# Gate and turn of a fused Mamba, BitLinear, attention and feed-forward kernel written out step by step, with the rounding of quantised rows on ScalarE

## The reference

```python
x = x + tanh(g_xattn[0]) * mamba(ctx, z=layernorm(x))       # scan over 16 states, then y * silu(z)
x = x + tanh(g_ffn[0])   * bitlinear_ffn(layernorm(x))      # w1, exact gelu, w2
x = x + tanh(g_xattn[1]) * attention(layernorm(x), ctx)     # softmax of q k^T over channels
x = x + tanh(g_ffn[1])   * ffn(layernorm(x))                # 2048 wide, exact gelu
# in bitlinear, per row of x:
scale = 127.0 / max(max(abs(x)), EPS)
x_quant = clip(round(x * scale), -128.0, 127.0) / scale
# in mamba, per channel and state n:
state = state * exp(dt * A) + (dt * u) * B;  y += state * C
```

## Time and profile before

| | us |
|---|---|
| median of 3 runs | 1057.2 (1055.8 to 1058.83) |
| the profiled execution | 1057.6 |
| its span, first to last instruction | 1055.8 |
| busy: TensorE, VectorE, ScalarE, GpSimd | 823.3, 824.9, 665.5, 564.1 |
| mean granted clock of TensorE, share of full | 0.896 |

### The profile page before, as it was taken

The page is one execution under the profiler, slowest core; times in us unless marked ns, Lnnn a source line. Parts: engine busy times, 40 slices in busy tenths (PEclk is TensorE's granted clock), DMA queues, the critical chain, the costliest instruction groups (busy, mean ns, idle before and its releaser), DMA issues.

```text
span 1055.8 us, 10904 instructions
## 1 busy us (share of the span) xinstructions
PE 823.3 (78%) x2704; PEld 399.7 (38%) x2704; DVE 824.9 (78%) x1001; ACT 665.5 (63%) x972; POOL 564.1 (53%) x493
## 2 busy tenths in 40 slices
PE   5442320699699987989699988889799988898998
PEld 2110110344334334444334334344333434445887
DVE  4879968887988897687998898777998897764333
ACT  4679969366589962365589962565599852533442
POOL 0398785123997783123997783134997782133000
PEclk9555555799899999998999999998999999999999
DMA  7069985001199897201199897201298995200222
GB/s 276 0 119 205 231 195 107 0 1 41 22 190 206 189 251 179 77 26 40 20 198 201 191 246 179 102 0 40 50 204 184 203 219 155 99 1 21 94 90 76
DMA packets 51439, 130.07 MB, mean 123 GB/s; under 512 B 6304, under 2 KB 7456, under 8 KB 50864
## 3 DMA queue, kind: packets, MB, share of 16 engines
q0 software_dynamic: 17280, 62.92, 32.4%
q1 hardware_dynamic: 34096, 66.53, 18.6%
HBM read 62.33 MB, written 4.19 MB: 63 GB/s over the span
## 4 chain that ended last, share of the span: by engine, by line
PE 27%; DVE 21%; issue 17%; ACT 13%; DMA 9%; POOL 8%; DVEq 1%; ACTq 0%; POOLq 0%
DMA u<-work 9%; DVE pair L1194 7%; PE bank L630 4%; PE pair L514 4%; PE pair L630 4%; POOL work L1600 4%; PE bank L615 3%; DVE pair L1207 3%; PE pair L542 3%; ACT pair L825 2%; ACT L825 2%; PE bank L602 2%; ACT L1074 2%; PE pair L591 1%; POOL u L1611 1%
## 5 line engine op out<-in xcount | busy, mean ns | idle before, releaser
L1600 POOL TENSOR_TENSOR work<-du,bcast 128x1024 f32<-128x1024 f32 x128 | 346.8, 2736 | 54.0 <-DVE du L1256 45.6
L825 ACT ACTIVATE pair<-dt,a_neg 128x512 f32<-128x512 f32 x256 | 166.3, 683 | 63.3 <-DVE work L1199 52.6
L1194 DVE TENSOR_TENSOR_SCAN pair<-pair,work 128x512 f32<-128x512 f32 x160 | 186.9, 1214 | 16.3 <-ACT pair L825 15.7
L602 PE MATMUL bank<-stage,ring 128*128 128x512 f32 x384 | 174.8, 598 | 11.0 <-ACT stage L1074 3.7
L1611 POOL DMA_DIRECT2D u<-work x120 | 126.0, 1050 | 67.6 <-DVE work L1211 22.4
L423 PE MATMUL bank<-xd,pick 128*128 128x512 bf16 x128 | 56.9, 445 | 101.9 <-ACT bcast L810 66.1
L1207 DVE TENSOR_TENSOR_SCAN pair<-pair,work 128x512 f32<-128x512 f32 x96 | 117.4, 1223 | 18.1 <-ACT pair L825 17.7
L602 PEld LDWEIGHTS bank<-stage,ring 128*128 128x128 f32 x384 | 70.4, 189 | 96.4 <-issue 78.5
L1199 DVE TENSOR_TENSOR work<-pair,ccast 128x1024 f32<-128x1024 f32 x80 | 98.0, 1225 | 11.4 <-DVE pair L1194 6.1
L615 PE MATMUL bank<-ring,stage 128*128 128x512 f32 x192 | 88.8, 614 | 8.4 <-DVE stage L1476 7.0
L423 PEld LDWEIGHTS bank<-xd,pick 128*128 128x128 bf16 x128 | 13.1, 103 | 161.7 <-ACT bcast L810 101.0
(11 more groups left out here) (181 smaller groups left out, 1606.9 us busy)
## 6 DMA issues: line engine op xcount, KB each, us to landing
u<-work POOLq DMA_DIRECT2D x120, 512.0 KB, 5.7
ring<-ffn_dram SPq DMA_DIRECT2D x144, 256.0 KB, 5.0
ring<-ffn_dram SPq DMA_DIRECT2D x16, 512.0 KB, 3.3
xres<-x_dram SPq DMA_DIRECT2D x4, 1024.0 KB, 5.2
stage<-w_dram SPq DMA_DIRECT2D x1, 4096.0 KB, 17.4
stage<-w_dram SPq DMA_DIRECT2D x4, 1024.0 KB, 6.8
out_dram<-stage SPq DMA_DIRECT2D x16, 256.0 KB, 2.1
ctxT<-ctxT_dram SPq DMA_DIRECT2D x4, 512.0 KB, 6.4
```

Of the source, the lines that this page charges most:

```text
L602: last = pe.matmul(banks[2 + f % 2][:], piece(f)[:, k * P:(k + 1) * P], xnT[:, k, :], start=k == 0, stop=k == J - 1)
L825: act.activation(pairs[s % DECAYBUFS][:, q, :], dt[:, p * HALF + q, :], ACT.Exp, scale=a_neg[:, p * HALF + q, n:n + 1]).then_inc(s_decay, 1)
L1194: dve.tensor_tensor_scan(pair[:, q, :], pair[:, q, :], rows[:, q, :], 0.0, ALU.mult, ALU.add).then_inc(s_scan, 1)
L1600: pool.tensor_tensor(work[:, s % SCANBUFS, :, :], du[:, p * HALF:(p + 1) * HALF, :], bcast[:, n % 2, :].unsqueeze(1).broadcast_to([P, HALF ...
```

## The change

Slots 13 and 14 go, and their contents are written out as `turning` (and `first_turning` for pass 0) on each engine. Of the steps: both sums of the gate stand ahead of both products; the rounding's multiply-add is made by ScalarE (`q_scale`) between VectorE's `q_norm` and `q_out`; `x1n` has two buffers, for even and odd tiles; the mean for the gate's norm is made by ScalarE (`gate_mean`), not GpSimd; `gate_transposes` of tile 3 stand behind a pair of `f_down`, and the transposes of `q1`'s tile 1 ahead of the last pair; ScalarE copies tiles 2 and 3 before the last gelu. In `between`, `h_quant(b, 0)` stands ahead of `convolve(m, 1)`, `attend(b, 1)` ahead of `norm_transpose(b, 2)`, with ScalarE's copy of that ahead of its first copy of B.

```diff
-SLOTS = 15
+SLOTS = 13
...
-            (12, 0): (1, 2), (12, 1): (1, 4), (12, 3): (1, 6),
-            (13, 0): (1, 8), (13, 2): (1, 10), (13, 3): (1, 12),
-            (14, 0): (1, 14)}
-FOURTH_SLOTS = {(11, 0): 0, (14, 1): 1}
+            (12, 0): (1, 2), (12, 1): (1, 4), (12, 3): (1, 6)}
+FOURTH_SLOTS = {(11, 0): 0}
...
-        x1n = ccast[:, 0, :]
+        x1n = ccast
...
+            def f_pair(b, r, f):
+                f_down(b, r, f)
+                f_down(b, r, f + 1)
+
+            def first_turning(m):
+                pe.wait_ge(s_wq, 4)
+                gate_transposes(m, (0, 1, 2, 3))
+                q_transposes(m, (0,))
+                up1(m, 0)
+                q_transposes(m, (1,))
+                up1(m, 1, range(FC - 1))
+                q_transposes(m, (2,))
+                up1(m, 1, (FC - 1,))
+                q_transposes(m, (3,))
+
+            def turning(b, m):
+                f_pair(b, 1, 8)
+                gate_transposes(m, (0,))
+                gate_transposes(m, (1,))
+                gate_transposes(m, (2,))
+                f_pair(b, 1, 10)
+                gate_transposes(m, (3,))
+                f_pair(b, 1, 12)
+                q_transposes(m, (0,))
                 up1(m, 0, range(FC - 1))
-                if prev is not None:
-                    f_unit(prev, QUANT_SLOT, 0)
+                q_transposes(m, (1,))
+                f_pair(b, 1, 14)
                 up1(m, 0, (FC - 1,))
-                q_transposes(m, (1,))
...
+                if t == 1 and m is not None:
+                    pe.wait_ge(s_spmax, m * J + J)
...
                 attend(b, 0)
+                attend(b, 1, m)
                 norm_transpose(b, 2)
                 scan_bcast(m, 0, 0)
-                attend(b, 1)
-                norm_transpose(b, 3)
                 attend(b, 2)
                 scan_bcast(m, 1, 0)
+                norm_transpose(b, 3)
...
+                norm_copy(b, 2)
                 first_copy(m, b, 0, 0)
-                norm_copy(b, 2)
...
+            def gate_mean(b, j):
+                act.wait_ge(s_zsum, b * J + j + 1)
+                act.activation(zst[:, j, 1:2], zst[:, j, 0:1], ACT.Copy, scale=-1.0 / D).then_inc(s_zmean, 1)
...
+            def q_scale(b, t):
+                act.wait_ge(s_q1s, b * T + t + 1)
+                act.activation(x1n[:, t % 2, :], x1n[:, t % 2, :], ACT.Identity, scale=mst[:, t, 12:13],
+                               bias=expo[:, 2:3]).then_inc(s_q1m, 1)
+
+            def turning(m):
+                q_scale(m, 0)
                 q_copy(m, (0,))
-                gelu1(m, 0)
+                q_scale(m, 1)
+                gelu1(m, 0, range(FC - 2))
+                q_scale(m, 2)
                 q_copy(m, (1,))
+                gelu1(m, 0, range(FC - 2, FC))
+                q_scale(m, 3)
                 gelu1(m, 1, range(FC - 1))
                 q_copy(m, (2,))
+                q_copy(m, (3,))
                 gelu1(m, 1, (FC - 1,))
-                q_copy(m, (3,))
...
                 convolve(m, 0)
+                h_quant(b, 0)
                 convolve(m, 1)
-                h_quant(b, 0)
...
+            def first_turning(m):
+                last_sum(m, 0)
+                last_sum(m, 1)
+                gated(m, 0)
+                gated(m, 1)
+                first_sum(m, 0)
+                first_sum(m, 1)
+                q_norm(m, 0)
+                first_sum(m, 2)
+                q_norm(m, 1)
+                q_out(m, 0)
+                first_sum(m, 3)
+                q_out(m, 1)
+                q_norm(m, 2)
+                q_norm(m, 3)
+                q_out(m, 2)
+                q_out(m, 3)
+
+            def turning(b, m):
+                last_sum(m, 0)
+                last_sum(m, 1)
+                gated(m, 0)
+                gated(m, 1)
+                first_sum(m, 0)
+                first_sum(m, 1)
+                first_sum(m, 2)
+                q_norm(m, 0)
+                q_out(m, 0)
+                first_sum(m, 3)
+                q_norm(m, 1)
+                q_out(m, 1)
+                q_norm(m, 2)
+                q_norm(m, 3)
+                fourth(b, 1)
+                q_out(m, 2)
+                q_out(m, 3)
...
-            def quantise(b, t):
+            def q_norm(b, t):
                 st = mst[:, t, :]
+                row = x1n[:, t % 2, :]
                 dve.wait_ge(s_x1rs, b * T + t + 1)
-                if t:
-                    dve.wait_ge(s_q1, b * T + t)
+                if t >= 2:
+                    dve.wait_ge(s_q1, b * T + t - 1)
...
-                dve_m.link(dve, b, dve.reciprocal(st[:, 12:13], st[:, 11:12]))
+                dve.reciprocal(st[:, 12:13], st[:, 11:12]).then_inc(s_q1s, 1)
                 dve.tensor_scalar(st[:, 13:14], st[:, 11:12], wstat[:, 0, 2:3], None, ALU.mult)
-                dve_m.link(dve, b, dve.tensor_scalar(x1n, x1n, st[:, 12:13], MAGIC, ALU.mult, ALU.add))
+
+            def q_out(b, t):
+                dve.wait_ge(s_q1m, b * T + t + 1)
                 if t >= 2:
                     dve.wait_ge(s_q1T, b * T + t - 1)
-                dve.tensor_scalar(q1[:, t % 2, :], x1n, MAGIC, 127.0, ALU.subtract, ALU.min).then_inc(s_q1, 1)
+                dve.tensor_scalar(q1[:, t % 2, :], x1n[:, t % 2, :], MAGIC, 127.0, ALU.subtract, ALU.min).then_inc(s_q1, 1)
...
-                if slot == ZSTAT_SLOT - 1:
-                    for j in range(J):
-                        pool.wait_ge(s_zsum, b * J + j + 1)
-                        carry_wait(pool, "pool")
-                        pool.tensor_scalar(zst[:, j, 1:2], zst[:, j, 0:1], -1.0 / D, 1.0, ALU.mult,
-                                           ALU.mult).then_inc(s_zmean, 1)
```

More of the change, by code:

```diff
@@ L54 @@
 ZS_SLOT = 12
-GATE_SLOT = 13
-QUANT_SLOT = 14
 W_MEAN = {5: 0, 10: 1}
@@ L279, in program @@
         s_q1 = sem("s_q1")
+        s_q1s = sem("s_q1s")
+        s_q1m = sem("s_q1m")
         s_q1T = sem("s_q1T")
@@ L746, in pass_ @@
                 for slot in range(4, SLOTS):
-                    if slot == QUANT_SLOT:
-                        turn(m, prev)
-                        continue
                     bcast_next(m, slot, 0, 0)
@@ L760, in pass_ @@
                         weights(slot)
-                    if slot == GATE_SLOT:
-                        gate_transposes(m, range(T))
                     bcast_next(m, slot, 0, 1)
@@ L778, in pass_ @@
                         f_unit(b, slot, 3)
+                if rest:
+                    turning(b, m)
+                else:
+                    first_turning(m)
             def weights(slot):
@@ L1127, in pass_ @@
                         gates_silu(m)
-                    if slot == QUANT_SLOT:
-                        turn(m)
+                turning(m)
             def weights(slot):
@@ L1520, in pass_ @@
                     half(m, prev, slot, 1, 1)
-                    mixer_last(m, prev, slot)
-                    if rest and (slot, 1) in FOURTH_SLOTS:
-                        fourth(b, FOURTH_SLOTS[slot, 1])
+                if rest:
+                    turning(b, m)
+                else:
+                    first_turning(m)
             pass_(None, rest=False)
@@ L1640, in mixer_last, with turning @@
                                            ALU.mult).then_inc(s_zrs, 1)
-                if slot == GATE_SLOT:
-                    for t in range(T):
-                        st = mst[:, t, :]
-                        pool.wait_ge(s_x1st, b * T + t + 1)
-                        rsqrt(pool_m, b, st[:, 8:9], st[:, 7:8], LN_EPS, st[:, 9:10], s_x1rs)
+            def turning(b):
+                for t in range(T):
+                    st = mst[:, t, :]
+                    pool.wait_ge(s_x1st, b * T + t + 1)
+                    rsqrt(pool_m, b, st[:, 8:9], st[:, 7:8], LN_EPS, st[:, 9:10], s_x1rs)
             def norm(b, i):
```

34 lines of the change are left out of this document (11 added, 23 removed).

## The result

| | kernel before | changed kernel |
|---|---|---|
| median, us (20 executions each) | 1056.49 (1051.71 to 1059.73) | 1059.33 (1055.32 to 1065.78) |
| ratio | | 1.0035, 95% interval 1.0019 to 1.0051 |
| profiled execution, and its span | 1057.6, 1055.8 | 1058.4, 1056.6 |
| mean granted clock in it | 0.896 | 0.888 |

The two profiled executions differ by only 0.8 us: each is one draw from a spread of several microseconds. So single steps can be compared, not the ends; a second profile of the changed kernel (e12) shows how far a stage scatters by itself.

What follows compares the result with a forecast made beforehand. No engine was taken to bound the whole; the bound changes by stage, with ScalarE's last start counting at batches 2 and 3. 0.5 + 1.9 + 0.1 + 0.3 - 0.4 + 0.4 = +2.8 us gave 1060.0 us, range 1054.5 to 1064.5.

Steps and rivals of the forecast that it cites:

- the gate's order: Gate, batches 2 to 4: product 0 leaves the DMA's wait for behind sum 1, so transposes come 1.25 us later.
- the moved transposes: TensorE's turn: tile 1's transposes ahead of the last f_down pair gain 1.29 us per batch in batches 2 and 4.
- batch 2, up to ScalarE's last start: Gate +1.25, TensorE's turn -1.29, last instruction now a gelu +0.50: ScalarE's last start moves by +0.5 us.
- batch 3: Either +1.7 us with new waits for VectorE's tiles at full clock, or +2.1 with the clock falling; +1.9 taken.
- batch 4: Gate +1.25 and turn -1.29 on TensorE, no loop return behind; VectorE's closing scale 1.2 us later: +0.1 us.
- batch 1 and the means: First batch: gate 1.05 us earlier but lost on VectorE, +0.3; gate's mean moved to ScalarE, -0.4 us.
- between the batches: h_quant(0) before the second convolution: zero; attention's second product ahead delays the third some 0.15 us, three times: +0.4 us.
- clock rival: Longer idle time ahead of the gate makes half clock last 3 us longer at batches 2 and 4: 1063.0 us; chance 0.20.
- the alternative: Batch 3: idle time before the gate, 2.68 now 3.9 us, lets TensorE's clock fall, hiding the new wait: +2.1 us.
- that rival: First batch: ScalarE's wait for the mean was the path, so 5.2 us are gained, not 0.4: 1055.2 us; chance 0.12.
- The rounding: Multiply-add on ScalarE: +0.5 us each for tiles 0 and 1 on VectorE's sequence; rival, every tile pays: 1064.1, chance 0.03.
- the return as a constant: Loop's return: ScalarE's last start to next unchanged near 4.4 us; rival, it changes: 1056.5 or 1063.5, chance 0.10.

Runs made afterwards that it cites:

- e12: The changed kernel once more, unaltered, for a second profile: 1058.61 us, span 1056.8.
- e1: Changed kernel with the gate of batches 2 to 4 back in the order sum 0, product 0, sum 1, product 1: median 1055.10 us, ratio 0.9990.
- e4: Changed kernel with the transposes of quantised tile 1 back behind the last f_down pair and last quarter, ScalarE's copy behind tile 0's gelus: median 1063.61 us, ratio 1.0080.
- e3: Changed kernel with the stretch between the batches back in its old order on all engines (hidden rows, attention, first copy of B): median 1056.64 us, ratio 1.0010.
- e10: Changed kernel with the passes written out and the old orders of gate (batches 2 to 4) and stretch between batches: median 1046.01 us, ratio 0.9887.
- e2: Changed kernel with the rounding's multiply-add made by VectorE at the end of the normalising step: median 1060.57 us, ratio 1.0045.
- e7: Changed kernel with only the first quantised hidden rows back behind the second convolution, attention in the new order: median 1057.62 us, ratio 1.0009.
- e8: Changed kernel, loop kept, with the edits of e1 and e3 together: median 1054.17 us, ratio 0.9988.
- e5: Changed kernel with the three passes written out on TensorE, ScalarE, VectorE and GpSimd, no hardware loop there: median 1048.63 us, ratio 0.9935.
- e9: The kernel before with its three passes written out instead of a loop: median 1050.42 us, ratio 0.9933.
- e11: e10 with 24 unused transposes of the identity put into TensorE's wait ahead of the gate of batches 2 to 4: median 1047.37 us, ratio 0.9895.

## Why the prediction was right, and where not

**Right in sum, and in the mechanism of its large terms.** The two are there, with opposite signs, and were found by undoing them: the gate's order +4.8 us (e1, give or take 3.0; forecast 3.75), the moved transposes -4.8 (e4, 3.7; forecast -3.9). Each batch by its steps, forecast against the first profile:

| | forecast | measured | of it |
|---|---|---|---|
| batch 2, up to ScalarE's last start | +0.5 | -0.8 | gate +1.0, turn -2.3, gelu last +0.5 |
| batch 3 | +1.9 | +2.0 | gate +1.0, turn +0.5, gelu last +0.5 |
| batch 4 | +0.1 | -0.2 | gate +1.0, turn -1.2 |
| batch 1 and the means | -0.1 | 0.0 | scan -0.5, gate -0.8, turn +1.3 |
| between the batches | +0.4 | +1.4 | the fall at 694 |

The measured steps add up to +2.4, but the two profiles lie only 0.8 apart: the other steps (the scan, the returns, the tail) differ by -1.6, and the forecast had put nothing on them. That these balance so in the medians is not shown.

*Gate order.* The mechanism is right. The size is 1.0, not 1.25: the products follow each other 1.13 us apart, closer than sum and product. The wait ahead of the gate was 5.51, 4.03 and 4.74 us in the first profile and 6.70, 5.34 and 5.02 in the second, where 7, 3.9 and 5.1 had been forecast. Its second effect, a longer wait that lets the clock fall, had been put only at the third batch and as an alternative. It fell there in both profiles. It held behind waits of 2.68, 3.27, 3.57 and 3.65 us (before, e1, e3) and fell in the kernel before behind 3.88 and 5.81; so did all six gates of batches 2 to 4 in the changed kernel's two profiles, behind 4.03 to 6.70. The wait alone doesn't decide: in e10 it fell behind one of 3.29. The clock rival of the prediction, a half clock that lasts 3 us longer in batches 2 and 4, did not come: the first quantised tile stood 10.45 and 10.35 us behind the gate, before 11.51 and 10.35.

*The turn.* -1.29 us was forecast and -1.2 measured from first to last transposes in batches 2 to 4. Batch 2 won 1.1 more, because TensorE stood at half clock for less of it than in the profile before. That is luck of the run.

*The third batch.* The new wait for VectorE's second tile, forecast at 1.1 us at full clock, did not show in the changed kernel, since its clock fell there; the +2.0 came by the alternative, priced at +2.1. In e1 and e3, with the clock up, the wait is 0.72 and 0.71. Its sum had a slip: 8.9 + 1.1 + 2.6 is 12.6, not 12.5, and a tile ready at 13.5 leaves 0.9. The first tile at 8.9 us: 8.82.

*The first batch and the means.* As forecast in each sign. The wait for the mean went to the wait for the weight's scale, 0.5 us sooner (forecast 0.6), and that rival is dead. Tile 0 was written at 195.69, slightly earlier than the 196.0 to 196.4.

*The rounding.* The extra 0.5 us per tile was a term only in the third batch. q_scale takes 0.81 us (0.77 by the nearest row). The Trainium skill, "ScalarE: Activation LUTs", Rules for kernel authors, sends add and mul to VectorE: the duration agrees with it (0.48 us there), the result doesn't; e2 puts the operation back on VectorE and is not faster.

**Wrong: between the batches.** The step "h_quant(0) before the second convolution lets TensorE transpose 1.2 us sooner, but TensorE already waits ...; VectorE's sequence keeps its sum. Zero" failed. It looked at the sum of the waits, not at their shape. Before, TensorE waited 1.25 us for the first tile and 1.26 for the second in passes 2 and 3. Now it doesn't wait for the first and waits 1.97 for the second: less in all, but longer in one piece, and in one pass of three the clock fell behind that. The +0.4 for attention's order was not seen by e3 against e7 (0.0001 apart).

**Wrong: the return as a constant.** "ScalarE's last start to its next unchanged near 4.4 us" assumed one time. It was 3.88 and 3.73 in the first profile, 3.12 and 4.74 in the second, and from 2.55 (e8) to 6.84 us (e4) in the others. That TensorE's product is not what it waits for is shown by e5, where it waits for just that and starts 1.28 us after its last start. On "Advanced Engine Details and Errata", Control Flow Timing, of the Trainium skill: about 108 ns for a compare-and-branch is not what a return of this loop costs; by e5 it costs some 3 us more than no return.

That the total came out within 0.7 us is luck in part, since misses cancel: the turn of batch 2 was 1.1 us better than forecast, the stretch between the batches 1.0 worse. The result's own interval, 2.0 to 5.4 us, would have fitted other sums as well.

## What to carry to other kernels

Put work that doesn't need the late data into the wait for it: a product that stood in the wait for a DMA cost nothing there, and a whole product (1.0 us a batch) behind it, and more where the engine behind then stood so long that its clock fell. When a step is moved, look for where an idle time of the next engine gets longer in one piece, not only at the sum of its idle times. A chain that crosses a loop's return should be tried without the loop before its order is tuned: that alone gave 0.7% on the kernel before and 1.0% on the changed one, more than any order here.

## What the runs showed of the hardware that was not expected

The return of a hardware loop took 4.8 to 9.1 us on the path (E), differing between two runs of the same code (6.10, 5.94 against 5.33, 6.95), while the same step in straight code took 3.49 or 3.50 us at each of the twelve places in e5, e9, e10 and e11. The scatter of the totals hangs on it only in part: the kernels without the loop still spread over 4 to 7 us (e5 1046.8 to 1052.9).

TensorE's clock could fall behind 1.97 us of waiting in one place and hold behind 3.65 us in another (the changed kernel between the batches, and e1 at its gate), and at one place it fell behind 1.97 us in some passes and held in others. Short dummy work ahead of the wait didn't hold it: in e11 it fell behind 24 narrow transposes and 1.95 us, and held behind the same and 1.33 us.
